# A recommendation tower on one core: where four small pieces of its written-out order stand

## What is computed

```
e = stack([tbl_f[ids[:, f]] for f in range(26)], axis=1)        # 2048 x 26 x 128
combined = concatenate([e, r_dense_x[:, None, :]], axis=1)      # 27 rows a sample
z = einsum('bfd,bgd->bfg', combined, combined)[:, I, J]         # 351 pairs, I < J
h = concatenate([z, r_dense_x], axis=1)                         # 479
h = maximum(h @ W_top1 + b_top1, 0)                             # 512
h = maximum(h @ W_top2 + b_top2, 0)                             # 256
y = h @ W_top3                                                  # 1
```

## Time and profile before

| | us |
|---|---|
| median of 3 runs | 358.85 |
| the profiled execution, its own time | 359.39 |
| its span in the profile | 357.7 |
| TensorE busy in the span | 336.0 |
| GpSimd busy | 250.0 |
| VectorE busy | 238.4 |
| ScalarE busy | 178.3 |

### The profile page before, as it was taken

The page is one execution under the profiler, slowest core; times in us unless marked ns, Lnnn a source line. Parts: engine busy times, 40 slices in busy tenths (PEclk is TensorE's granted clock), DMA queues, the critical chain, the costliest instruction groups (busy, mean ns, idle before and its releaser), DMA issues.

```text
span 357.7 us, 12506 instructions
## 1 busy us (share of the span) xinstructions
PE 336.0 (94%) x5576; PEld 278.2 (78%) x5576; DVE 238.4 (67%) x440; ACT 178.3 (50%) x238; POOL 250.0 (70%) x265
## 2 busy tenths in 40 slices
PE   7998899797999999999999999999999999998976
PEld 7787777676878788877888788787888788977864
DVE  2999989774378856787468784787587793430322
ACT  3898534381617634283535735176344827363412
POOL 6788777777777777777777777777777777777000
PEclk9999999998999999999999999999999999999999
DMA  6988683333343343335253334333443322222000
GB/s 222 369 238 268 171 245 87 87 82 99 71 111 84 86 99 100 85 81 118 64 121 96 82 99 93 88 83 88 100 97 88 94 55 56 66 54 55 24 2 3
DMA packets 19657, 37.67 MB, mean 105 GB/s; under 512 B 5557, under 2 KB 8501, under 8 KB 19604
## 3 DMA queue, kind: packets, MB, share of 16 engines
q1 hardware_dynamic: 11412, 20.09, 20.0%
q0 software_dynamic: 8192, 16.79, 18.6%
HBM read 36.85 MB, written 0.01 MB: 103 GB/s over the span
## 4 chain that ended last, share of the span: by engine, by line
PE 72%; DVE 19%; issue 4%; ACT 2%; DMA 2%; SPq 0%; DVEq 0%; ACTq 0%
PE ps_lk L638 26%; DVE onehot L336 15%; PE ps_gram L664 14%; PE ps_tr L649 8%; PE ps_zt L691 7%; PE ps_mlp L691 6%; PE ps_zt L698 3%; PE ps_mlp L698 3%; DVE table L347 3%; PE ps_lk L711 2%; DMA ids<-in_ids_onehot 2%; PE ps_zt L678 1%; PE ps_lk L726 1%; ACT ids L440 0%; ACT xt L460 0%
## 5 line engine op out<-in xcount | busy, mean ns | idle before, releaser
L294 POOL DMA_INDIRECT rows<-in_tbl,gather_ids x256 | 248.7, 971 | 79.7 <-issue 76.2
L336 DVE TENSOR_SCALAR onehot<-ids 128x513 fp32r<-128x513 f32 (+3 forms) x328 | 179.9, 621 | 40.1 <-PE ps_lk L638 24.0
L638 PE MATMUL ps_lk<-onehot,table 128*128 128x512 f32 (+1 forms) x720 | 160.8, 375 | 4.5 <-DVE onehot L336 1.8
L638 PEld LDWEIGHTS ps_lk<-onehot,table 128*128 128x128 f32 x720 | 121.2, 188 | 29.7 <-DVE onehot L336 3.7
L469 ACT COPY xt<-ps_tr 128x512 f32<-128x512 f32 x64 | 77.2, 1207 | 98.5 <-PE ps_tr L649 98.5
L664 PEld LDWEIGHTS ps_gram<-xt 128*26 128x26 f32 x4096 | 44.1, 103 | 24.5 <-issue 22.6
L664 PE MATMUL ps_gram<-xt 128*26 128x26 f32 x4096 | 53.4, 192 | 9.7 <-issue 6.3
L355 DVE STREAM_TRANSPOSE zs<-ps_gram 128x832 f32<-128x832 f32 x16 | 16.8, 1050 | 62.4 <-PE ps_gram L664 62.4
L448 ACT COPY xt<-ps_lk 128x512 f32<-128x512 f32 x32 | 38.5, 1244 | 9.2 <-PE ps_lk L638 5.2
L649 PE MATMUL ps_tr<-ident,rows 128*128 128x128 f32 x256 | 40.3, 280 | 1.1 <-DMA rows<-in_tbl,gather_ids 0.8
L649 PEld LDWEIGHTS ps_tr<-ident,rows 128*128 128x128 f32 x256 | 30.0, 142 | 7.5 <-issue 1.6
(11 more groups left out here) (62 smaller groups left out, 142.3 us busy)
## 6 DMA issues: line engine op xcount, KB each, us to landing
ids<-in_ids_onehot SPq DMA_DIRECT2D x41, 258.0 KB, 3.7
rows<-in_tbl,gather_ids POOLq DMA_INDIRECT x256
w<-in_tbl SPq DMA_DIRECT2D x6, 512.0 KB, 8.8
h<-in_tbl SPq DMA_DIRECT2D x2, 512.0 KB, 6.8
zt<-in_tbl SPq DMA_DIRECT2D x2, 512.0 KB, 6.5
dense_x<-in_dense SPq DMA_DIRECT2D x8, 128.0 KB
zt<-in_dense SPq DMA_DIRECT2D x8, 128.0 KB, 2.5
w<-in_w SPq DMA_DIRECT2D x1, 512.0 KB
```

The source lines that it names most:

```text
L294: pool.indirect_dma_start(rows[n % ROW_BUFS][:, r, :], None, t_[f"tbl_{GATHERED[r]}"], bass.IndirectOffsetOnAxis(ap=gather_ids[:, n, r:r + ...
L336: nc.vector.tensor_scalar(to, of.bitcast(F32), float(k), None, ALU.is_equal).then_inc(s_unit, 1)
L638: m = nc.tensor.matmul(ps_lk[e % LB][:, x], table[:, i, part, k, :], onehot[:, k, x], start=(k == 0 and j == 0 and part == 0), stop=(k == ...
```

## The change

It has these parts:

- The ids of step 0 are loaded from ScalarE's DMA queue, not as the second transfer of SyncE's. The warm-up products are 15, not 20.
- Step 8, the first of chunk 1, compares plain ids as the steps of chunk 0 do (`in_thirds`).
- The twelfth step (step 11, `SPARE`) goes to layer 1's bank `ps_mlp`, and it stands between the two parts of gram(1); the later steps use the three `ps_lk` banks one place earlier. ScalarE's and VectorE's order around it follows.
- `lookup(5)` stands ahead of `turn(0, 3)`.
- `gram` states its wait for `s_turned` first, which places that wait on gram's first matmul; the others are carried by wait instructions before it.
- At the end, the gram of tile 15 is in one piece, after three parts of `last1`, `turn(15, 3)` and `layer2`.

```
-WARM_UP = 20
+WARM_UP = 15
+def in_thirds(e):
+    return e > STEP0[1]
...
+        SPARE = STEP0[1] + LB
+        def lookup_bank(e):
+            return ps_mlp if e == SPARE else ps_lk[(e if e < SPARE else e - 1) % LB]
...                                                  # SyncE
-            load_ids(0)
...                                                  # VectorE
             make_units(STEP0[1] + 3)
             row_constants()
-            pack(1)
             for c in range(1, CHUNKS - 1):
                 make_units(STEP0[c] + 4)
+                if c == 1:
+                    pack(1)
...                                                  # ScalarE, first instruction
+            act.dma_start(ids[0][:, :], t_["ids_onehot"][0:1, :].to_broadcast([P, IDS_W])).then_inc(s_ids[0], 16)
...                                                  # TensorE
-                if e >= LB and ks[0] == 0:
-                    pe.wait_ge(s_lk, e - LB + 1)
+                if e >= LB and e != SPARE and ks[0] == 0:
+                    pe.wait_ge(s_lk, e - LB if SPARE < e <= SPARE + LB else e - LB + 1)
...
                 if part == 0:
+                    pe.wait_ge(s_turned, (n + 1) * NGR)
                     pe.wait_ge(s_lk, STEP0[n // CT + 1])
-                    pe.wait_ge(s_turned, (n + 1) * NGR)
...
             lookup(4)
+            lookup(5)
             turn(0, 3)
-            lookup(5)
             lookup(6)
...
             turn(2, 0)
+            lookup(e + 3)
+            turn(2, 1)
             gram(1, 1)
...                                                  # the end
             layer2(c - 1, 0)
-            layer2(c - 1, 1)
             turn_pairs(a)
-            turn(a + 1, 3)
             last1(0, 0)
             last1(0, 1)
+            last1(0, 2)
+            turn(a + 1, 3)
+            layer2(c - 1, 1)
             gram(a + 1, 0)
-            last1(0, 2)
+            gram(a + 1, 1)
             last1(0, 3)
-            gram(a + 1, 1)
-            last2(0, (0, 1, 2))
             for j in range(LB):
                 dense_rows(1, j, True)
+            last2(0, (0, 1, 2))
```

More of the change, by code:

```diff
@@ L80 @@
 UNIT_W = N + 16
+def in_thirds(e):
+    return e > STEP0[1]
 def cols_of(e):
-    c, w, tables = STEPS[e]
+    _, w, tables = STEPS[e]
     n = w * P * len(tables)
-    if c == 0:
+    if not in_thirds(e):
         return list(range(n))
@@ L102 @@
 FIRST_PARTS = 2
-WARM_UP = 20
+WARM_UP = 15
 LAST = (CHUNKS - 1) * MLP_USES
 LAST_ACT = (CHUNKS - 1) * T1
+LAST_BUT = (CHUNKS - 1) * CT
 def build(nc, t_, out):
@@ L374, in finish @@
                 m, t = divmod(n, CT)
-                dve.wait_ge(s_mlp, m * MLP_USES + T1 + t + 1 if m < CHUNKS - 1 else last(t + 1))
+                dve.wait_ge(s_mlp, LAST + LB if n == LAST_BUT - 1 else
+                            m * MLP_USES + T1 + t + 1 if m < CHUNKS - 1 else last(t + 1))
                 if n == 0:
@@ L436, in shift @@
                 w = cols_of(e)[-1] + 1
-                if STEPS[e][0] > 0:
+                if in_thirds(e):
                     w = THIRDS * (-(-STEPS[e][1] * P * len(STEPS[e][2]) // THIRDS) + 1)
@@ L447, in evac @@
                 if w == XT:
-                    nc.scalar.copy(xt[:, :, a], ps_lk[e % LB][:, :]).then_inc(s_lk, 1)
+                    nc.scalar.copy(xt[:, :, a], lookup_bank(e)[:, :]).then_inc(s_lk, 1)
                 else:
@@ L485, in last_relu1 @@
             def last_relu1(t, j):
-                act.wait_ge(s_mlp, last(t) + j + 1)
+                act.wait_ge(s_mlp, last(t) + j + (0 if t == 0 and j < LB else 1))
                 nc.scalar.activation(h1[:, j, t * P:(t + 1) * P], last1_bank(t, j), ACT.Relu, bias=cols[:, j:j + 1]
                                      ).then_inc(s_act, 1)
+            act.dma_start(ids[0][:, :], t_["ids_onehot"][0:1, :].to_broadcast([P, IDS_W])).then_inc(s_ids[0], 16)
             act.wait_ge(s_first, 1)
@@ L517, in _ @@
             evac(4)
-            evac_group(0, 3)
             shift(7)
@@ L521, in _ @@
             evac(5)
+            evac_group(0, 3)
             shift(8)
@@ L535, in _ @@
             evac_new(STEP0[1] + 2)
+            shift(STEP0[1] + 4)
             evac_zt(0)
             evac_group(2, 0)
+            evac_group(2, 1)
             act.wait_ge(s_cols, 16)
@@ L545, in _ @@
                     evac_old(e)
-                    shift(e + 4)
                     evac_old(e + 1)
+                    evac_group(a, 2)
+                    shift(e + 5)
+                    evac_old(e + 2)
+                    evac(e + 3)
                     evac_zt(a - 1)
-                    evac_group(a, 1)
-                    evac_old(e + 2)
                     evac_dense(c)
+                    evac_group(a, 3)
+                    evac(e + 4)
+                    relu1(c - 1, 0)
                 else:
@@ L561, in _ @@
                     evac(e + 2)
-                evac(e + 3)
-                shift(e + 5)
-                if c == 1:
-                    evac_group(a, 2)
-                evac(e + 4)
-                relu1(c - 1, 0)
-                if c == 1:
-                    evac_group(a, 3)
+                    evac(e + 3)
+                    shift(e + 5)
+                    evac(e + 4)
+                    relu1(c - 1, 0)
                 shift(e + 6)
@@ L636, in lookup @@
                         for part in range(2):
-                            m = nc.tensor.matmul(ps_lk[e % LB][:, x], table[:, i, part, k, :], onehot[:, k, x],
+                            m = nc.tensor.matmul(lookup_bank(e)[:, x], table[:, i, part, k, :], onehot[:, k, x],
                                                  start=(k == 0 and j == 0 and part == 0),
@@ L718, in dense_rows @@
             def dense_rows(t, j, first):
+                if first:
+                    pe.wait_ge(s_act, last_act(t - 1) + j + 1)
                 return nc.tensor.matmul(last1_bank(t, j), w1[:, NZ, j * P:(j + 1) * P], zt[:, NZ, t * P:(t + 1) * P],
@@ L764, in _ @@
                 a, e, f = c * CT, STEP0[c], STEP0[c + 1]
-                if c > 1:
-                    turn(a, 3)
-                lookup(e + 3)
-                turn_pairs(a - 1)
-                if c == 1:
-                    turn(a, 1)
-                lookup(e + 4)
                 if c == 1:
                     turn(a, 2)
+                    lookup(e + 4)
+                    turn_pairs(a - 1)
+                    turn(a, 3)
+                    lookup(f)
                     pe.wait_ge(s_cols, 16)
@@ L776, in _ @@
                     pe.wait_ge(s_w, 16 * 4)
-                layer1(c - 1, 0)
-                if c == 1:
-                    turn(a, 3)
-                    lookup(f)
+                    pe.wait_ge(s_lk, SPARE + 1)
+                    layer1(c - 1, 0)
                     gram(a, 0)
                 else:
+                    turn(a, 3)
+                    lookup(e + 3)
+                    turn_pairs(a - 1)
+                    lookup(e + 4)
+                    layer1(c - 1, 0)
                     gram(a, 0)
```

10 lines of the change are left out of this document (5 added, 5 removed).

## The result

The changed kernel takes 364.64 us (median of 4 runs, 364.04 to 366.1) against 358.77 us for the kernel before (median of 4, 357.24 to 359.21). The ratio is 1.0177, with a 95% interval of 1.0132 to 1.0222: it is slower by 5.9 us, where 2.0 us of gain were forecast and 358.7 us was the upper end of the range. The profiled execution took 365.19 us, its span is 363.5 us.

The account below looks back on a forecast made before the run. TensorE was taken to bound the kernel, with time to gain only before 113 us or after 318. Terms of 1.6 (cap), 0, 0.2 (packet edges) and 0.2 (end) sum to 2.0 us: 358.85 becomes 356.9, range 355.0 to 358.7.

Parts of the forecast that it names:

- What bounds the kernel: Whole run: TensorE, busy 336.0 of 357.7 us; the change must earn its time before 113 us or after 318.
- First ids: Start: ids issued from ScalarE's queue come about 0.4 us earlier (0 to 0.45), and the tables behind them too.
- Fewer warm-up products: nothing: Start: no gain, as they end before the first lookup has data; packet edges move by 20 instructions.
- Lookup(5), step 8 plain, step 11: Before gram(2, 0): with the earlier ids, TensorE is 3.5 us ahead there, and the 1.40 us stand goes.
- The cap: At turn(4, 3), gathered rows limit TensorE's lead to 1.6 us (0.8 to 2.1), gathers coming 0.4 us later.
- s_turned on gram's matmul: In gram: it moves one wait and no work, 0 (-0.5 to +0.5).
- Packet edges, +0.2: From 113 to 336 us: shifted instruction-packet edges lose and make stands, a gain of 0.2 us (-2 to +1.2).
- Rival D: Loop's grams: new packet edges bring stands of 1.2 to 2.2 us, with slow clock if long; slower, chance 0.09.
- The end: Last tile: last pairs turned 1.7 us earlier, less 1.5 for pack's cover and stands: +0.2 us (-1.0 to +1.7).
- A: At turn(4, 3): TensorE idles 1.4 to 3 us and the clock falls to 1.2 GHz, 358.2 us; chance 0.18.
- C: Start and gathers: ids compete with GpSimd's list, cap at 0.5, end even: no gain, 358.3 to 358.9; chance 0.11.

Follow-up runs that it names:

- e7: The kernel before with 15 warm-up products instead of 20, nothing else: 362.53 us, ratio 1.0102.
- e4: The changed kernel with step 0's ids back on SyncE's queue and the end as before: 358.50 us, ratio 0.9978 to the kernel before.
- e5: e4 with 20 warm-up products instead of 15: 360.41 us, ratio 1.0034 to the kernel before.
- e1: The changed kernel with step 0's ids back on SyncE's queue, behind the gather list: 362.40 us, ratio 1.0100 to the kernel before.
- e17: e4 with gram's waits in the old order, s_lk on the first matmul and s_turned separate: 357.96 us, ratio 0.9973 to the kernel before.
- e11: e4 with 25 warm-up products instead of 15: 360.72 us, ratio 1.0042 to the kernel before.
- e12: The kernel before with the new end, but turn(15, 3) ahead of the turn of pairs 14: 359.42 us, ratio 1.0030.
- e13: The changed kernel with turn(15, 3) ahead of the turn of pairs 14: 361.77 us, ratio 1.0082 to the kernel before.
- e14: e1 with turn(15, 3) ahead of the turn of pairs 14: 360.64 us, ratio 1.0034 to the kernel before.
- e18: The kernel before with gram's two waits exchanged, s_turned on the first matmul and s_lk separate: 360.48 us, ratio 1.0043.
- e8: The changed kernel with step 0's ids issued from ScalarE only once GpSimd's gather list has landed: 365.16 us, ratio 1.0166 to the kernel before.
- e6: The kernel before with the new end alone: 363.48 us, ratio 1.0140.

## Why the prediction was wrong

**What bounds the kernel**: right. The time was lost before 113 us and after 318 us, but for 0.6 us.

**First ids**: this step failed. VectorE did start earlier, by 0.5 us in the mean of the profiles where 0.4 was taken. "May push GpSimd's first list back by some tenths" was the term that mattered, and it was 2.5 us: the list landed 4.6 us after its issue, in the kernel before 2.0. It fell on the chain that I had myself called free of slack; undoing it gave 2.2 us (0.8% by the ratios).

**Fewer warm-up products: nothing**: wrong in the kernel before, which e7 made 1% slower (0.3 to 1.8%); right in that it has no sign of its own, since e4 with 15 is 0.6% faster than e5 with 20. The edges are the part that the profiles bear out, the clock in e7's first lookup another of unknown size.

**Lookup(5), step 8 plain, step 11**: right in mechanism, of no clear worth under the cap. Lookup 8 ended 2 us earlier (gram(0,0) at 44.96 in e4, 47.02 before), the 1.40 us in gram(1,1) went, and in e5 gram(2,0) started 0.2 us from the forecast. With 15 products the stand in gram(0,0) and the clock behind it ate this lead at once: in e4 gram(2,0) starts at 81.90 us, as in the kernel before.

**The cap**: right as a mechanism. With the ids undone TensorE waited 1.59 to 1.85 us for rows, at 112.3 to 112.5 us; the turn stood 0.3 to 0.6 us ahead of before in e4 and e1, 1.7 in e5, for a forecast of 1.6. In e1 and e4 the gathers came 0.5 and 1.0 us later, not 0.4; but the end of gather 80 scatters from 109.02 to 110.50 us over the fifteen profiles with the ids on SyncE, so a lead read from one profile is good to about a microsecond. Of the 1.6 us that it was to give, e4 shows 0.2% (0 to 0.5%).

**s_turned on gram's matmul**: taken as 0 (-0.5 to +0.5), it was +1.8 in the kernel before (and nothing clear in the changed one, e17). I weighed which wait ends last and not what a separate wait holds up behind it.

**Packet edges, +0.2**: right in kind, not in sign: the new stand of 1.34 us in gram(8,0) came mostly from the wait's place. Rival D named stands in the loop's grams with the clock behind them. In the changed kernel's profile there is one, without the clock; in e4 and e5 one with it, in e11 two (207.79 and 293.41 us), not three.

**The end**: this step failed too, and it is the largest miss, +0.2 forecast, -4.6 measured. The sum priced each piece moved and not the bank: layer 2's second part was the cover of `finish`. The exposed 1.20 us, the clock behind it (4.57 - 2.94 = 1.6 us), and the copy of turn (15,3), now late enough to hold back the packet in the gram, make the loss; by e12 and e13, where moving that turn alone gives back 4.1 and 2.9 us and leaves 0.77 us of the wait, the turn's place is the larger part. The sum counted the turn as 0.45 us of work and not as the start of a copy that the gram needs. That the long gram meets a stand was right. (Pack's cover is 0.9 us too long by its own rows, 3.3 - 2.4, not 1.1; the sum doesn't use it.)

**Rivals**: A (1.2 GHz after the wait at the cap) happened in e5 and e14, in the changed kernel not (a wait of 1.49 us). C had the right cause, the ids against the list, but priced it too low. None held an exposed wait at the end.

The Trainium skill (Runtime: NRT & Kernel Launch, Instruction fetch mechanics) calls the cost of crossing a block mostly hidden. The trace agrees for most crossings: of the 44 packets of the kernel before, all but six cost less than 0.3 us. It does not for those six, which cost 0.3 to 2.2 us each, and e18 shows one that a wait's place makes.

## What to carry to other kernels

When a piece of work is moved, ask which bank or buffer its neighbours now meet unready: the piece may have been the cover of another engine's last read. Two transfers issued together on two queues (128 and 258 KB here) are not free of each other; issue the one that feeds a chain without slack first and the other right behind it. Holding the other back until the first has landed gained nothing here (e8). Of several waits ahead of a long run of short matmuls, put the one that is met last on the matmul itself (shown at gram(8,0)), and above all turn its source early.

## What the hardware showed that I had not expected

A list of 128 KB issued at 0.81 us beside a 258 KB transfer of another queue let its first reader start at 5.26 to 5.99 us, without it at 3.1 to 3.3. At gram(8,0) a packet of instructions started 1.0 to 2.0 us after the separate wait was met, and its instructions ran 2.3 to 2.9 us after its start (206.89 and 209.48 in e18): the gram stood for 1.3 to 2.5 us. The granted clock fell to 1.2 GHz for 3.4 us after many idles of 1.75 to 2.9 us and not after all (one of 2.56 us in e1, ahead of the first lookup, had no fall behind it), and after two shorter ones close together, 1.20 and 0.62 us at the end of the changed kernel, but not after the same two in e6.
